# Value rows of the last batch made during the first scan and kept in DRAM, scan products summed in pairs in four rounds

## The reference, cut to what matters

```
V = ctx @ Wv            # per batch (512, 2048): heads in 8 groups of 2
O = softmax(Q K^T / sqrt(128)) V
y_t = sum_n state[t, :, n] * C[t, n]
```

## Time and profile before

| | us |
|---|---|
| median of 3 runs | 1864.55 (1863.48 to 1865.01) |
| the profiled execution's own time | 1868.66 |
| its span | 1867.0 |
| TensorE busy | 1773.8 (95%) |
| VectorE busy | 1206.2 (65%) |
| ScalarE busy | 1087.6 (58%) |
| GpSimd busy | 261.7 (14%) |

### The profile page before, as it was taken

How to read it: one execution, slowest core, us unless ns; L and a number is a source line. 1 busy time by engine, 2 the same in 40 slices (tenths; PEclk the granted TensorE clock), 3 DMA queues, 4 the chain that set the end, 5 groups by cost and what they waited for, 6 DMA issues and landing times.

```text
span 1867.0 us, 26032 instructions
## 1 busy us (share of the span) xinstructions
PE 1773.8 (95%) x8314; PEld 1133.9 (61%) x8346; DVE 1206.2 (65%) x1549; ACT 1087.6 (58%) x2450; POOL 261.7 (14%) x250
## 2 busy tenths in 40 slices
PE   8899999999999999999999999999889999988898
PEld 4455545767765476766645676775457767644453
DVE  6999778977875798777678977776452010124542
ACT  5767457766754775666557766664555555445350
POOL 0002111000101010000101100010031101105570
PEclk9999999999999999999999999999999999999999
DMA  7355312323231122323122222323134332402535
GB/s 227 102 170 161 110 42 68 97 80 106 77 86 63 56 99 85 90 79 95 64 81 74 82 85 86 95 79 118 46 130 85 80 77 67 95 15 82 142 118 180
DMA packets 112891, 176.03 MB, mean 94 GB/s; under 512 B 11936, under 2 KB 64416, under 8 KB 112304
## 3 DMA queue, kind: packets, MB, share of 16 engines
q1 hardware_dynamic: 97776, 157.20, 27.4%
q0 software_dynamic: 14224, 16.28, 4.1%
q10 hardware_dynamic: 816, 1.57, 0.3%
HBM read 146.29 MB, written 35.02 MB: 97 GB/s over the span
## 4 chain that ended last, share of the span: by engine, by line
PE 79%; DVE 9%; ACT 6%; issue 4%; POOL 1%; DMA 0%; ACTq 0%; DVEq 0%; SPq 0%; POOLq 0%
PE ps L1980 27%; PE pp L1980 18%; PE px L1980 17%; PE pd L1980 6%; PE po L1980 5%; DVE arena L1516 3%; DVE arena L1508 2%; PE pp L2336 1%; ACT hbuf L1277 1%; PE pd L2307 1%; PE po L2307 1%; POOL xg_dram L903 1%; DVE arena L1527 1%; DVE fsc L1680 1%; PE ps L2176 1%
## 5 line engine op out<-in xcount | busy, mean ns | idle before, releaser
L1516 DVE TENSOR_TENSOR_SCAN arena<-arena 128x512 f32<-128x512 f32 x256 | 292.2, 1203 | 4.2 <-ACT arena L1016 3.6
L1277 ACT ACTIVATE hbuf<-ps,shift,rms_k 128x512 f32<-128x512 f32 x256 | 198.6, 777 | 123.1 <-PE ps L1980 115.6
L1980 PE MATMUL ps<-qkT_rows 128*128 128x512 f32 x512 | 250.7, 601 | 6.7 <-ACT hbuf L1277 2.8
L1980 PE MATMUL pp<-wq,xnT 128*128 128x256 f32 x1024 | 236.7, 386 | 2.9 <-issue 2.2
L1980 PEld LDWEIGHTS pp<-wq,xnT 128*128 128x128 f32 x1024 | 193.8, 194 | 29.1 <-ACT xnT L1232 4.3
L831 POOL TENSOR_TENSOR rms<-ssv,minus_half 128x4 f32<-128x4 f32 x64 | 82.0, 1281 | 863.6 <-ACT ssv L1253 863.6
L1016 ACT ACTIVATE arena<-arena,a_neg 128x512 f32<-128x512 f32 x256 | 163.7, 722 | 0.0
L1980 PEld LDWEIGHTS po<-v_ext,hbuf 128*128 128x128 f32 x768 | 105.9, 191 | 61.2 <-issue 61.2
L1980 PEld LDWEIGHTS ps<-qkT_rows 128*128 128x128 f32 x512 | 82.2, 190 | 83.6 <-ACT hbuf L1277 58.2
L1508 DVE TENSOR_TENSOR arena<-arena,bc 128x2048 f32<-128x2048 f32 x56 | 126.3, 2287 | 6.7 <-issue 5.6
L1735 DVE TENSOR_TENSOR xc<-xc,px 128x512 f32<-128x512 f32 x64 | 43.4, 678 | 134.3 <-PE px L1980 134.3
(11 more groups left out here) (339 smaller groups left out, 3002.8 us busy)
## 6 DMA issues: line engine op xcount, KB each, us to landing
bc<-bc_dram SPq DMA_DIRECT2D x56, 512.0 KB, 5.5
wo<-in_Wo SPq DMA_DIRECT2D x32, 512.0 KB, 3.6
wq<-in_Wq SPq DMA_DIRECT2D x32, 512.0 KB, 3.6
qkT_rows<-kt_dram SPq DMA_DIRECT2D x32, 512.0 KB, 4.5
hbuf<-in_w SPq DMA_DIRECT2D x8, 1024.0 KB, 9.6
wv<-in_Wv SPq DMA_DIRECT2D x32, 256.0 KB, 2.9
wk<-in_Wk SPq DMA_DIRECT2D x25, 256.0 KB, 3.1
kt_dram<-xnT SPq DMA_DIRECT2D x12, 512.0 KB, 2.6
```

The costliest lines, as they stand in the source:

```text
L1277: nc.scalar.activation(pT[:, h, k], ps[s_use % 2][:], ACT.Exp, bias=shift[:, 0:1], scale=rms_k[:, bass.ds(G * (GH * NT) + (h * NT + k), 1) ...
L1516: V.tensor_tensor_scan(hb[i][:, e], dA[i][:, e], hb[i][:, e], 0.0, ALU.mult, ALU.add).then_inc(scan_done[i], 1)
L1980: return nc.tensor.matmul(out, lhsT, rhs, start=first, stop=last, **kw)
```

## The change

The value rows of all 8 groups of batch 3 (`V_BATCH`) are made in rounds 4 and 5 of the first scan as units V0 to V7, copied to the key units' stage buffers and stored in a new DRAM tensor `v_dram`. A table `WORK` gives the units of each round in their order. A V unit has 16 pieces of 256 columns on the banks pp; the weights come by turns into `wv` and `wk`. The context is now changed to batch 3's behind K9 and to batch 0's behind V7. In batch 3's groups `v_rows` and their copies are gone, and SyncE loads the value rows of the next group into `v_ext` once the group's last values are done.

In rounds 3 to 6 (`PAIRED`) VectorE adds the two products `hc_first[0]` and `hc_first[1]` (`pair_c`), and TensorE adds one sum for both (`y_pair`), behind the unit that `PAIR_BEHIND` names: K8, V1, V7 and K12. In rounds with more than one unit the ternary transposes stand behind the second unit. SyncE treats the round's first unit, then loads the broadcast rows and the ternary weights, and then treats the other units.

```diff
+V_BATCH = 3
+WORK = [
+         [("K", 2)],
+         [("K", 3), ("K", 4)],
+         [("K", 5), ("K", 6)],
+         [("K", 7), ("K", 8), ("K", 9)],
+         [("V", 0), ("V", 1), ("V", 2), ("V", 3), ("V", 4)],
+         [("V", 5), ("V", 6), ("V", 7), ("K", 10)],
+         [("K", 11), ("K", 12), ("K", 13)],
+         [("K", 14), ("K", 15)],
+]
+PAIRED = (3, 4, 5, 6)
...
+            def v_dma(m):
+
+                sp.wait_ge(pp_full[1], v_at(m))
+                if m + 2 < NG:
+                    wv_ahead(m + 2)
+                elif m % 2 == 0:
+                    w_load("v", 0)
+                else:
+                    w_load("k", first_unit(KEYS_BEFORE[m])[1])
+                    ctx_load(0)
+                for j in range(2):
+                    sp.wait_ge(pp_drained[j], v_at(m) + 1)
+                sp.dma_start(v_dram[m], v_stage_first[V_STAGE[m]]).then_inc(k_stored[V_STAGE[m]], 16)
+
+            def v_load(g):
+
+                sp.dma_start(v_sb, v_dram[bass.ds(g, 1)].rearrange("o p t h d -> p (o t) h d")).then_inc(v_in, 16)
...
             for r in range(TC):
-                for n in round_units(r):
-                    first_dma(n)
+                front_dma(*WORK[r][0])
                 if r + 2 < TC:
                     for i in range(GH):
                         sp.wait_ge(hc_done[i], r + 2)
...
                     w_stage(r + 4, r % 2, 2)
+                for kind, n in WORK[r][1:]:
+                    front_dma(kind, n)
...
                         kt_load(G + 1)
+                        if b == V_BATCH:
+                            bank, n = d_at(turn_, g, GH - 1)
+                            sp.wait_ge(px_full[bank], n)
+                            v_load(g + 1)
...
+            def first_v_out(m):
+
+                stage_ = V_STAGE[m]
+                act.wait_ge(k_stored[stage_], 16 * ((KEYS_BEFORE[m] + 1 - stage_) // 2 + V_STAGE[:m].count(stage_)))
+                for j in range(2):
+                    act.wait_ge(pp_full[j], v_at(m))
+                    nc.scalar.activation(v_stage_first[stage_][:, 2 * j:2 * j + 2], pp[j][:].rearrange("p (t h d) -> p t h d", t=2, h=GH),
+                                         ACT.Copy).then_inc(pp_drained[j], 1)
...
+                for at_, (kind, n) in enumerate(WORK[r]):
+                    if kind == "K":
+                        first_out(n)
+                    else:
+                        first_v_out(n)
+                    for i in range(GH):
+                        if at_ == 0 and r + 1 < TC and not r == i == 0:
+                            decay(0, r + 1, i)
+                        if at_ == 1 and r + 2 < TC:
+                            tern(w_out, r + 2, range(2 * i, 2 * i + 2))
+                        if kind == "K":
+                            first_sums_out(n, i)
...
+            def pair_c(r):
+
+                for i in range(GH):
+                    dve.wait_ge(hc_done[i], r + 2)
+                V.tensor_tensor(hc_first[0], hc_first[0], hc_first[1], ALU.add).then_inc(hc_paired, 1)
...
+            def y_pair(r):
+
+                pe.wait_ge(hc_paired, PAIRED.index(r) + 1)
+                for e in range(EC):
+                    m = mm(y_first[e][:], ident[:], hc_first[0][:, e], False, True, skip_group_check=True)
+                m.then_inc(y_added, GH)
...
+                for j in range(2):
+                    pe.wait_ge(pp_drained[j], v_at(m))
+                    for i in range(2):
+                        k = 2 * j + i
+                        for c in range(CC):
+                            last_ = mm(pp[j][:, i * GW:(i + 1) * GW], ctx_att[:, c, k * P:(k + 1) * P], w[:, c], c == 0, c == CC - 1)
+                    last_.then_inc(pp_full[j], 1)
...
+                for at_, (kind, n) in enumerate(WORK[r]):
+                    if kind == "K":
+                        for h in range(GH):
+                            first_k(n, h)
+                    else:
+                        first_v(n)
+                    if r in PAIRED and at_ == PAIR_BEHIND[r]:
+                        y_pair(r)
+                    for i in range(GH):
+                        if at_ == 0 and r not in PAIRED and not r == i == 0:
+                            y_sum(r, i)
+                        if at_ == 1 and r + 2 < TC:
+                            tern(r + 2, range(2 * i, 2 * i + 2))
+                        if kind == "K":
+                            first_sums(n, i)
...
-                        v_rows(0)
-                        v_rows(1)
+                        if b != V_BATCH:
+                            v_rows(0)
+                            v_rows(1)
```

More of the change, by code:

```diff
@@ L101 @@
 U_FIRST = G_FIRST * (B - 1)
+V_BATCH = 3
[10 more added lines that the diff above has]
+PAIRED = (3, 4, 5, 6)
+PAIR_BEHIND = {r: max([1] + [i for i, item in enumerate(WORK[r]) if item == ("V", NG - 1)]) for r in PAIRED}
+ITEMS = [("K", 0), ("K", 1)] + [item for items in WORK for item in items]
+assert [n for kind, n in ITEMS if kind == "K"] == list(range(U_FIRST + 1)) and [n for kind, n in ITEMS if kind == "V"] == list(range(NG))
+KEYS_BEFORE = [sum(kind == "K" for kind, _ in ITEMS[:ITEMS.index(("V", m))]) for m in range(NG)]
+VALUES_BEFORE = [sum(kind == "V" for kind, _ in ITEMS[:ITEMS.index(("K", n))]) for n in range(U_FIRST + 1)]
+V_STAGE = [(k + KEYS_BEFORE[:m].count(k)) % 2 for m, k in enumerate(KEYS_BEFORE)]
+CTX_FRONT = B if V_BATCH == B - 1 else B - 1
 K_OFF = {"KT": 0, "SS": 2}
@@ L523, in first_unit, with ctx_after @@
             return n, G_FIRST if n == U_FIRST else FIRST_BATCHES[n // G_FIRST] * NG + n % G_FIRST
+        def ctx_after(n):
+            return V_BATCH if V_BATCH == B - 1 and n == KEYS_BEFORE[0] - 1 else FIRST_BATCHES[n // G_FIRST + 1]
         def stored_by(end, parity):
-            return 16 * ((end + 1 - parity) // 2)
+            return 16 * ((end + 1 - parity) // 2 + V_STAGE[:values_before(end - 1)].count(parity))
         U_EARLY = 2
[L530 to L535, removed]
         def for_batches(turn):
@@ L1124, in _ @@
             for r in range(TC):
-                units = round_units(r)
                 if 0 < r < TC - 2:
                     tern(w_sums, r + 2)
[L1128 to L1135, removed]
+                for at_, (kind, n) in enumerate(WORK[r]):
[10 more added lines that the diff above has]
+                            first_sums_out(n, i)
+                if len(WORK[r]) == 1 and r + 2 < TC:
                     tern(w_out, r + 2, range(0, 2))
-                for n in units[1:]:
-                    first_sums_out(n, 0)
-                if r + 2 < TC:
                     tern(w_out, r + 2, range(2, 4))
-                for n in units[1:]:
-                    first_sums_out(n, 1)
                 if r == TC - 2:
@@ L2330, in v_rows, with v_drained @@
                         m.then_inc(v_full[j], 1)
+                    def v_drained():
+                        for j in range(2):
+                            pe.wait_ge(v_out[j], v_turn(G) + 1)
                     def q_turned(h):
@@ L2351, in values @@
                     def values(h, k):
-                        for j in range(2):
-                            pe.wait_ge(v_out[j], G + 1)
+                        if b == V_BATCH:
+                            pe.wait_ge(v_in, g * 16 + 16)
+                        else:
+                            v_drained()
                         pe.wait_ge(ones_set, b + 1)
```

92 lines of the change are left out of this document (56 added, 36 removed).

## The result

The changed kernel takes 1874.86 us (median of five executions, 1873.72 to 1879.0), the kernel before 1865.01 (1863.48 to 1865.23) beside it: slower, 1.0053 with a 95% interval of 1.0042 to 1.0064, or +9.85 us. The profiled execution of the changed kernel was the slowest of its five, 1879.0 for a span of 1877.3; against the profiled one of before that is +10.3.

What follows compares the result with a forecast made beforehand. VectorE paced the front before; TensorE's chain was to bound it after. Longer chain +22.8, clock +8.5 and context load +1.0, less 25.5 in the last batch, gave net +6.8 us: 1871.4 us, range given 1860 to 1880.

Steps and rivals of the forecast that it cites:

- The bound: First scan: VectorE paces its rounds before the change but does not stay the bound; TensorE's chain then sets the front.
- second rival: Front stays bound by VectorE: its price 14.3 us, net -11.2, 1853.4 us; chance 0.16.
- The chain on TensorE: Front, laid out unit by unit: first `scan_end` transposes at 246.0 us against 223.18, +22.8 before clock and context load.
- The change of context: On TensorE before V0 and before K10: 5.25 us each from the unit before to the next.
- The clock: Front: waits bring falls to half clock at 1.7 us each; five taken, 8.5 us, bounds 0 and 11.9.
- my six places: Front: places with waits where the clock might fall, before K8, V0, ternary 7, K11, K12 and K14.
- first rival: The clock holds in the front: with no fall net -1.7, with one 0.0, 1864.6 us; chance 0.22.
- The load of the next context: End of the front: ScalarE's load has a lead of 2.7 us and wants about 3.5: +1.0, bounds 0 and 2.5.
- third rival: Front: value units paced by DMA, each about 4.2 us: +5 on the forecast, 1876.4 us; chance 0.16.
- The last batch, -25.5: Batch 3 without its value rows: groups 1 to 7 gain 3.46 us each, group 0 gains 1.3.
- The sum: Whole kernel: front +32.3, last batch -25.5, net +6.8 us, 1871.4 us on the median.
- SyncE's order, 0: First scan: broadcast rows and weights ahead of the second unit's store move loads nothing waits for, 0 us.

Runs made afterwards that it cites:

- e4: Changed kernel without pairing (`PAIRED = ()`), so TensorE sums both products in rounds 3 to 6: 1884.85 us, 1.0101 of the kernel before.
- e6: Kernel before with pairing alone in rounds 3 to 6, no value rows moved: 1874.90 us, 1.0052 of the kernel before.
- e3: Changed kernel with ScalarE copying the small sums before the decays in rounds 3 and 6: 1872.99 us, 1.0036 of the kernel before.
- e9: Changed kernel run again with no edit: 1876.70 us, 1.0058 of the kernel before.
- e11: Changed kernel with three unread 128x512 matmuls in batch 3's first group in place of the value rows: 1876.56 us, 1.0050 of the kernel before.
- e2: Changed kernel with unread 128x512 matmuls added in the waits before K10, K11, K12 and K14: 1874.14 us, 1.0037 of the kernel before.
- e5: Kernel before with batch 3's value rows, their copies and their loads left out: 1842.06 us, 0.9878 of the kernel before.
- e10: Kernel before with only the change's SyncE order: 1867.30 us, 1.0001 of the kernel before.
- e12: Changed kernel with round 3's small sums copied earlier, two sums moved into waits, `gate_silu` earlier, unread matmuls in waits: 1866.51 us, 1.0006 of the kernel before.

## Why the prediction was right, point by point

- **The bound.** Right. The front turned from VectorE's to TensorE's: VectorE waits 16.56 us before `gate_y`, pairing saves 8 to 9 us in e4 and costs 8 to 9 in e6. The second rival (front stays VectorE's, 1853) falls by both.
- **The chain on TensorE.** Right in its places, 2 to 4 us too long in the sum. From K7 to the first transpose I laid out 121.4 us without falls; the two estimates give 117.2 to 119.5. The waits stand where they were put: ScalarE's small copies before K8 and K12 (1.63 each, 0.7 of it left in e3), reloads (0.65 after 0.48), contexts (2.43 and 2.59), ternary 7 paced by ScalarE (5.06 for 5.4). Their sizes were off in parts. K8 and K12 start 4.1 us behind the end of the unit before them, for 4.9. The change of context was put at 5.25 both times from the earlier trace rows, but there TensorE was idle for only 1.0 of it, the rest being ternary work and small sums; before V0 it took 4.9 us, and 3.7 and 3.8 in e9 and e11, and before K10 6.2, 5.7 and 5.6.
- **The clock.** The price of a fall was right in the first profile (5.4 us for a unit instead of 3.7), but not in all: in e9 and e11 fallen units took 4.8 to 6.7. That TensorE's idleness brings the falls was shown by e2. The number was taken as five, and there were six, four and five; by length times clock these three executions lost 10.4, 8.8 and 13.0 us for the 8.5 of the sum. K10 fell in two of them and was not among my six places; the place at ternary 7 showed in one, at V7. The first rival (the clock holds, 1864.6) falls: in no trace of this front did it hold. A chain laid out too long and a clock priced too low stand against each other, so that the front came out close (first transpose 254.5 by the prediction; 255.01, 250.66 and 254.51 measured) is in part luck.
- **The load of the next context.** Right, and larger. `scan_a` is 1.4 us later than the transposes account for (33.3 against 31.8), for 1.0, and it is the load: issued at 255.19, it landed 4.1 us later, 0.2 before `scan_a` starts. In e9 it took 5.1 us and in e11 3.5, and `scan_a` starts again 0.2 behind the landing. From the first transpose to `scan_a` that is 4.45, 5.45 and 3.89 us, for 3.02 before, so 1.4, 2.4 and 0.9.

```profile
255.19 0.45 ACTq L1170 DMA_DIRECT2D dsum<-in_ctxT  x1
```
- **Value units paced by DMA.** The third rival falls: they follow at 3.5 us, here and in every experiment, with a wait of 0.3 to 0.8 us before one of the eight in some profiles. The value units' weight loads landed in a median of 4.3 us (four into `wk`) and 3.2 (four into `wv`), for 2.9 for the loads of key weights into `wk`. The four issued between 172 and 183 us, each while the store before it was on its way, took 3.3, 3.2, 3.2 and 3.9.
- **The last batch, -25.5: the step that failed.** Groups 1 to 7 gave 3.45 each, as said. Group 0 was to give 1.3 and gave -0.15. The transposes do come 1.36 us earlier, as predicted (10.45 us behind the first query rows, 11.81 before), but TensorE's wait ahead of them grows from 1.20 to 3.30 us and takes the clock with it: they take 1.97 us for 1.24, and the scores 3.75 for 1.96. e5 shows it without the rest of the change, e11 gives the 1.4 us back by keeping TensorE busy. It is the same mechanism that I had priced in front and not looked for here.
- **The sum.** +6.8 predicted, +9.85 and +9.6 measured. The missing 3 (3.5 in the first profile): 1.5 is group 0. The rest is, in that profile, 1.0 in front, 1.5 in batches 0 to 2 and -0.5 in the tail; the clock falls at other places there, but what each fall costs wasn't measured. Single executions differ by more than this rest: up to `scan_a` the front is 33.3 us longer in the first profile, 29.9 in e9 and 32.2 in e11.
- **SyncE's order, 0.** Right (e10).

## What to carry to other kernels

Work moved from one full engine-stage to another is worth the difference of what it costs in both places, and the waits around it count, not the work alone: here 13.6 us of net work cost some 30, because the new seams brought waits, and most of these a fall of the clock, not the same ones each time. Before such a move, look at what stands in each seam (a single weight buffer, one-column sums, a context load) and put useful work there first. And a wait that appears where work is taken out can eat the gain: look for it at both ends of the move.

## What was not expected of the hardware

- The 3.1 us before K11 (one-column sums with waits of 0.48 and 0.65 us) were enough for a fall to the 1.2 GHz level in the first profile and not in e9; a wait of 2.59 us was enough before K10, and one of 2.09 in e9 was not. The same code fell at K8, K12 and K14 in all three executions, at K10 and K11 in two, at V0 and V7 in one. A unit that fell took 4.8 to 6.7 us instead of 3.7.
- Matmuls whose result nobody reads kept the granted clock at 1.00 for 50 us (e2), and shortened group 0 by 1.4 us in e11.
- In e6, where VectorE set the pace, four key units fell to half clock, and VectorE did not wait for them.
- Single executions scatter by more than most of the remedies are worth: e12's twelve went from 1863.16 to 1872.92 us, those of the kernel before beside it from 1863.36 to 1868.30.
